# Routing two batches at once, every other iteration of the attention loop

## What is computed

```python
x = x + xattn(layernorm(x), ctx, mask, ...)      # q and o: quantized linear layers; k and v: plain
h = layernorm(x)                                 # 3584 tokens
probs = softmax(h @ router_w.T)                  # E = 8 experts
vals, idx = top_k(probs, 2); vals /= vals.sum()  # two experts for each token
x = x + sum over the two of vals * (silu(h @ gate.T) * (h @ up.T)) @ down.T
```

## Time and profile before

| | us |
|---|---|
| median of three runs | 1626.49 |
| the profiled execution | 1627.48 |
| its span (first to last instruction) | 1625.8 |
| PE busy | 1506.3 (93%) |
| DVE busy | 944.7 (58%) |
| ACT busy | 878.9 (54%) |
| POOL busy | 731.8 (45%) |
| mean granted clock of PE | 0.974 |

### The profile page before, as it was taken

The page is one execution under the profiler, slowest core; times in us unless marked ns, Lnnn a source line. Parts: engine busy times, 40 slices in busy tenths (PEclk is TensorE's granted clock), DMA queues, the critical chain, the costliest instruction groups (busy, mean ns, idle before and its releaser), DMA issues. The chain is left out here.

```text
span 1625.8 us, 40635 instructions
## 1 busy us (share of the span) xinstructions
PE 1506.3 (93%) x11593; PEld 1312.3 (81%) x11594; DVE 944.7 (58%) x2675; ACT 878.9 (54%) x2128; POOL 731.8 (45%) x798
## 2 busy tenths in 40 slices
PE   2899999999999999999999999995299999999796
PEld 2788888888888888888888888874299999999695
DVE  6567777777777777777777777765222222222121
ACT  2466666666666666666666666664033333333232
POOL 4234444543445434543444434542445555555352
PEclk9999999999999999999999999997599999999898
DMA  6667777677667777677766776668147766575543
GB/s 201 171 171 204 202 207 184 176 220 199 188 178 193 208 201 185 175 219 197 192 180 188 213 201 187 175 178 264 33 77 181 184 162 142 141 171 121 134 78 46
DMA packets 219151, 281.53 MB, mean 173 GB/s; under 512 B 82080, under 2 KB 163872, under 8 KB 219104
## 3 DMA queue, kind: packets, MB, share of 16 engines
q1 hardware_dynamic: 200928, 247.78, 54.2%
q0 software_dynamic: 18176, 33.17, 11.4%
HBM read 118.12 MB, written 66.77 MB: 114 GB/s over the span
## 5 line engine op out<-in xcount | busy, mean ns | idle before, releaser
L500 ACT ACTIVATE probs<-probs,neg_max 112x375 f32<-112x375 f32 x512 | 311.8, 609 | 235.2 <-DVE neg_max L576 229.1
L576 DVE CUSTOM_DVE_ANT_0 probs<-score,neg_mask 112x375 f32<-112x375 f32 x512 | 279.3, 545 | 195.9 <-PE score L729 179.7
L493 ACT ACTIVATE probs_t<-turn 125x336 f32<-125x336 f32 x512 | 225.0, 440 | 99.8 <-PE turn L737 99.4
L737 PE MATMUL turn<-ident,probs 112*125 112x112 f32 x1536 | 265.7, 282 | 2.7 <-ACT probs L500 2.7
L737 PEld LDWEIGHTS turn<-ident,probs 112*125 112x125 f32 x1536 | 223.6, 189 | 37.6 <-issue 19.1
L729 PE MATMUL score<-k_stack,q_stack 96*112 96x376 f32 x512 | 208.5, 407 | 4.3 <-DMA q_stack<-q_lo 3.4
L764 PE MATMUL proj<-down_hi,gate_up_hi 128*128 128x376 f32 x512 | 176.2, 344 | 14.9 <-DVE gate_up_lo L601 13.7
L978 POOL DMA_INDIRECT out<-y_rows,entries x63 | 102.2, 1622 | 175.0 <-ACT y_rows L1004 136.9
L1016 DVE TENSOR_TENSOR a_lo<-a_ps,a_hi 128x384 fp32r<-128x384 f32 x63 | 35.1, 558 | 250.9 <-ACT a_hi L991 159.0
L764 PE MATMUL proj<-down_hi,gate_up_lo 128*128 128x376 f32 x512 | 172.1, 336 | 0.0
L764 PE MATMUL proj<-down_lo,gate_up_hi 128*128 128x376 f32 x512 | 172.0, 336 | 0.0
(11 more groups left out here) (195 smaller groups left out, 3552.7 us busy)
## 6 DMA issues: line engine op xcount, KB each, us to landing
k_stack<-gate_up_hi SPq DMA_DIRECT2D x512, 94.0 KB, 2.1
k_stack<-gate_up_lo SPq DMA_DIRECT2D x256, 94.0 KB, 2.1
ctx_stage<-ctx_t SPq DMA_DIRECT2D x32, 750.0 KB
q_stack<-q_hi SPq DMA_DIRECT2D x256, 56.0 KB, 2.0
w_raw<-gate_up_t SPq DMA_DIRECT2D x32, 352.0 KB, 3.1
gate_up_dram_hi<-w_hi SPq DMA_DIRECT2D x32, 352.0 KB
gate_up_dram_lo<-w_lo SPq DMA_DIRECT2D x32, 352.0 KB
gate_up_hi<-gate_up_dram_hi SPq DMA_DIRECT2D x16, 704.0 KB, 6.6
```

Source lines behind the costliest of these rows:

```text
L493: act.activation(probs_t[:, h % RING_T, :, :], turn[h % 2][0:LC, 0:LT * N].rearrange("p (l n) -> p l n", l=LT), ACT.Copy).then_inc(turned_ ...
L500: act.activation(probs[:, h % DS, :], probs[:, h % DS, :], ACT.Exp, bias=neg_max[:, par % 2, h:h + 1], scale=-1.0, accum_out=total[:, par ...
L576: dve.tensor_tensor_reduce(probs[:, h % DS, :], score[h % 2][0:N, 0:L], neg_mask[:, p, :], 1.0, BIG, ALU.add, ALU.min, neg_max[:, p, h:h + ...
L737: mm = pe.transpose(turn[h % 2][0:LC, l * N:(l + 1) * N], probs[:, h % DS, l * LC:(l + 1) * LC], W["ident"][0:N, 0:N])
```

## The change

Routing is done for a pair of batches (an even one and the odd one after it) in the odd iterations. In each iteration DVE still finds the ordered logits and `equal` of its batch, now in one half of tiles that are twice as large. Everything behind that (L613 to L642 on DVE, L793 and L794 on PE, L439 to L482 on POOL, L541 on ACT) is left out of even iterations and done with twice the elements in odd ones. `taken_sum` now has two halves, the count before the even batch and the count before the odd one, so one more DVE addition stands at h = 8, behind `taken`. L619 and L634 compare with a broadcast tile in place of a scalar. The indirect DMAs aren't widened: an odd iteration issues four of them, an even one none. The two rank matmuls load 128 columns of weights in place of 112 and stream 16 columns in place of 8.

```diff
-                if has_m2:
-                    need(pool, routed, ROUTE * m2 + 1)
-                    need(pool, grown_made, m2)
-                    pool.tensor_tensor(gap[:, :], ordered[:, 1:2], ordered[:, 0:1], ALU.subtract).then_inc(weighing, 1)
+                if has_m2 and par % 2:
+                    need(pool, top_made, 2 * pair + 2)
+                    need(pool, grown_made, pair)
+                    pool.tensor_tensor(gap[:, :], ordered[:, :, 1], ordered[:, :, 0], ALU.subtract).then_inc(weighing, 1)
...
-                if has_m2:
...
-                    for i in range(2):
-                        pool.indirect_dma_start(slots, bass.IndirectOffsetOnAxis(ap=at[:, i:i + 1], axis=0), entry[:, i, :], None).then_inc(entered, 16)
+                if has_m2 and par % 2:
...
+                    for b in range(2):
+                        for i in range(2):
+                            pool.indirect_dma_start(slots, bass.IndirectOffsetOnAxis(ap=at[:, b, i:i + 1], axis=0), entry[:, b, i, :], None).then_inc(entered, 16)
...
-                    if h == 8 and has_m2:
-                        need(dve, routed, ROUTE * m2 + 6)
-                        dve.tensor_scalar(one[:, 1, :], W["prio"][0:N, :], best[1][:, 0:1], None, ALU.is_equal).then_inc(routed, 1)
-                        need(dve, routed, ROUTE * m2 + 7)
-                        need(dve, ranked, m2)
-                        dve.tensor_tensor(taken[0:N, :], one[:, 0, :], one[:, 1, :], ALU.add).then_inc(routed, 1)
-                    if h == 12 and has_m2:
-                        need(dve, routed, ROUTE * m2 + 9)
-                        need(dve, entered, 32 * m2)
-                        dve.tensor_reduce(at[:, :], chosen[:, :, :], AX.X, ALU.max).then_inc(routed, 1)
-                        dve.tensor_tensor(taken_sum[:, :], taken_sum[:, :], taken[0:N, :], ALU.add).then_inc(routed, 1)
+                    if h == 8 and has_m2 and par % 2:
+                        prio2 = W["prio"][0:N, :].unsqueeze(1).to_broadcast([N, 2, E])
+                        need(dve, routed, ROUTE * pair + 5)
+                        dve.tensor_tensor(one[:, :, 1, :], prio2, best[1][:, :].unsqueeze(2).to_broadcast([N, 2, E]), ALU.is_equal).then_inc(routed, 1)
+                        need(dve, routed, ROUTE * pair + 6)
+                        need(dve, ranked, pair)
+                        dve.tensor_tensor(taken[0:N, :, :], one[:, :, 0, :], one[:, :, 1, :], ALU.add).then_inc(routed, 1)
+                        need(dve, routed, ROUTE * pair + 7)
+                        dve.tensor_tensor(taken_sum[:, 1, :], taken_sum[:, 0, :], taken[0:N, 0, :], ALU.add).then_inc(routed, 1)
+                    if h == 12 and has_m2 and par % 2:
+                        need(dve, routed, ROUTE * pair + 9)
+                        need(dve, entered, 64 * pair)
+                        dve.tensor_reduce(at[:, :, :], chosen[:, :, :, :], AX.X, ALU.max).then_inc(routed, 1)
+                        dve.tensor_tensor(taken_sum[:, 0, :], taken_sum[:, 1, :], taken[0:N, 1, :], ALU.add).then_inc(routed, 1)
...
-                    if h == 11 and has_m2:
-                        need(pe, routed, ROUTE * m2 + 8)
+                    if h == 11 and has_m2 and par % 2:
+                        need(pe, routed, ROUTE * pair + 8)
                         if has_a:
                             need(pe, masked, it * H + h - 1)
-                        pe.matmul(rank[0:N, :], W["before"][0:N + 1, 0:N], taken[0:N + 1, :], start=True, stop=False)
-                        pe.matmul(rank[0:N, :], W["ones16"][0:N, 0:N], taken_sum[:, :], start=False, stop=True).then_inc(ranked, 1)
+                        pe.matmul(rank[:, :], W["before"][0:N + 1, :], taken[0:N + 1, :, :].rearrange("p b e -> p (b e)"), start=True, stop=False)
+                        pe.matmul(rank[:, :], W["ones16"][0:N, :], taken_sum[:, :, :].rearrange("p b e -> p (b e)"), start=False, stop=True).then_inc(ranked, 1)
```

More of the change, by code:

```diff
@@ L274, in attention @@
         NTP = NT + NT % 2
[L275 to L280, removed]
+        ordered, second = sb("ordered", [N, 2, E]), sb("second", [N, 2, E])
+        equal, weighed = sb("equal", [N, 2, 2, E]), sb("weighed", [N, 2, 2, E])
+        best = [sb(f"best{i}", [N, 2]) for i in range(2)]
+        one, taken, taken_sum = sb("one", [N, 2, 2, E]), W["taken"], W["taken_sum"]
+        chosen, at = sb("chosen", [N, 2, 2, E]), sb("at", [N, 2, 2], I32)
+        gap, grown, grown1 = sb("gap", [N, 2]), sb("grown", [N, 2]), sb("grown1", [N, 2])
+        entry = sb("entry", [N, 2, 2, 2], I32)
         cnt_i, tiles, last, jump = sb("cnt_i", [128, E], I32), sb("tiles", [128, E]), sb("last", [128, E]), sb("jump", [128, E])
@@ L283, in attention @@
         place_i = sb("place_i", [128, NTP], I32)
-        rank = score[1][:, LP:LP + E]
+        rank = score[1][:, LP:LP + 2 * E]
         o_bank, o_bank16 = proj[0], proj[1][:, :].bitcast(BF16)
@@ L416, in _, with body @@
         def _(pool):
-            def body(it, par, inside=False):
+            def body(it, par, pair, inside=False):
                 has_m2, has_m, has_a, has_n, has_nn, _ = stages(it, inside)
@@ L475, in body @@
[L475 to L479, removed]
+                    need(pool, weighing, WEIGH * pair + 4)
@@ L617, in body @@
[L617 to L623 removed]
+                        need(dve, routed, ROUTE * pair + 1)
@@ L699, in _ @@
             dve.wait_ge(counted, 1)
-            table(1, dve.tensor_scalar(cnt_i[:, :], rank[:, :], float(SLOTS - 1), float(SLOTS), ALU.add, ALU.max))
+            table(1, dve.tensor_scalar(cnt_i[:, :], rank[:, 0:E], float(SLOTS - 1), float(SLOTS), ALU.add, ALU.max))
             table(2, dve.tensor_scalar(cnt_i[:, :], cnt_i[:, :], 7, None, ALU.arith_shift_right))
@@ L856, in _ @@
             iterations(pe, body)
-            pe.wait_ge(routed, ROUTE * B)
-            pe.matmul(rank[:, :], W["ones16"][0:N, :], taken_sum[:, :], start=True, stop=True).then_inc(counted, 1)
+            pe.wait_ge(routed, ROUTE * B // 2)
+            pe.matmul(rank[:, 0:E], W["ones16"][0:N, :], taken_sum[:, 0, :], start=True, stop=True).then_inc(counted, 1)
 EXPERT_DMAS = 8
```

93 lines of the change are left out of this document (51 added, 42 removed).

## The result

The changed kernel took 1724.01 us (median of 4 runs, 1721.84 to 1737.63), beside 1627.39 for the kernel before: 1.061 times as long, with a 95% interval of 1.055 to 1.067. The forecast was 1670 with a range of 1640 to 1698. The sign was right and the size less than half of what was measured: +43 us predicted, +97 measured.

The account below looks back on a forecast made before the run. PE was taken to wait for `k_lo` behind POOL's DMAs. +2.6 us a pair gave +36.3 over 14 pairs; with -0.7 for early starts, -3.4 tail and +11 clock, +43 us: 1670 us, range 1640 to 1698.

Parts of the forecast that it names:

- What bounds the kernel: PE waits for DVE's `k_lo` 28 times, 13.7 us, behind POOL's DMAs; `o_int` has no slack before PE's turn.
- Two DMAs moved: Two more DMAs on POOL in odd iterations delay the next L425 by 2.68 us a pair; bounds 0 and 2.68.
- signs of being wrong: Wrong if L425 doesn't follow the DMAs, `k_lo` isn't PE's wait, or PE's period is no longer than before.
- DVE at head 8: New addition behind `taken` waits for POOL's L447, making `o_int` 1.25 us later; +0.3 us a pair, bounds 0 and 1.25.
- the two stalls don't add up: PE's 1.25 us stall at `o_int` and its later meeting with POOL's routing chain were not to be paid together.
- Wider operations on POOL: Entry operations on POOL with two elements a partition instead of one: +0.1 us a pair.
- Start of odd iterations: No DMA ahead of L425, so it starts 1.2 us sooner and `k_lo` is nearly in time: -0.35 us, bounds 0 and -0.55.
- PE −0.14 a pair: Even iterations lack the rank matmuls between PE's turn behind `values` and the score: -0.14 us, bounds -0.1 and -0.2.
- 128 columns nothing: Rank matmuls' weight loads on PE take 99 ns, not 136; at most 0.07 us ahead of a wait, so nothing.
- The tail: Iteration 33's L425 starts 4.87 us sooner, against four DMAs (+2.68 us): -3.4 us, bounds -2.2 and -4.7.
- The clock: PE's clock drops behind some waits at head 4 of even iterations: 0.8 us a pair, +11 us; bounds 0 and 3.4 a pair.
- no rival: Four alternatives: clock stays up, 1659 us (0.27); heavier, 1707 (0.08); DMAs don't hold L425, 1614 (0.07); half, 1641 (0.13).

Follow-up runs that it names:

- lower level: Runs of paired kernels in sets 2, 4 and 5, without late uptake of PE's results; the changed kernel took 1679.01 us (ratio 1.032).
- upper level: The first result and sets 1 and 3: ACT or DVE takes up a PE result over 1.5 us late once a pair; changed kernel 1724.01 us.
- sets 1 and 4: Groups of kernels run on one chip beside the kernel before, which took 1628.12 us in the first of them and 1625.51 in the other.

## Why the prediction was right or wrong

**What bounds the kernel: right.** A wait of PE behind POOL's queue, and `o_int` without slack. Moving the DMAs out of the way of the first gave 17 us; the earlier trace rows has 13.7.

**Two DMAs moved, +2.68 us a pair: right mechanism, wrong place in the sum.** The kernel before with doubled DMAs shows it: `x_s` 0.01 us behind the fourth, `k_lo` late by 3.05 us. The pitch was 1.25 us for the added ones, not 1.34. But in the changed kernel the term of 2.68 us is not paid in the pairs: `y` came after the DMAs. Two of the prediction's own signs of being wrong came true: L425 doesn't follow the DMAs, and `k_lo` isn't PE's wait.

**DVE at head 8, +0.3 us a pair: this is the step that failed.** The prediction had the addition's own wait right (1.18 us, ending with L449; 1.1 to 1.2 was forecast) and its way through `c_hi` and head 12 too. Counted from the start of the query bias, `o_int` starts 1.26 us later than before and `w_lo` 0.31 us later; the prediction had 1.25 and 0.3. It didn't put the two side by side. In before, `o_int` ran 0.3 us ahead of POOL's L461; with these two delays it starts behind L461's start, lasts 2.51 us in place of 0.43, and PE waits 3.2 us. So the stall of 1.25 us, which was the term's upper bound and was taken as mostly hidden, is one of 3.2 us, 15 times. The argument "the two stalls don't add up" was right; which of them is paid was reversed. The extra addition in the kernel before shows the cause by itself: 4.1 us an iteration.

The Trainium skill (SBUF — State Buffer, "SBUF: two separate sides") says that whichever of the two engines starts first has the shared ports for the whole instruction and the other blocks fully, and it counts operations in a 2-port mode among them, not only those with two inputs. `o_int` has one SBUF input; its 2.51 us agree with that half of the rule, which the prediction did not apply. Applied to the rows of before, with the prediction's delay of 0.3 us, `w_lo` ends at 921.59 + 0.3 + 2.47 = 924.36 and `o_int` not earlier, so that PE's turn of 921.33 is some 3.0 us late: an estimate, beside the measured 3.2.

**Wider operations on POOL, +0.1: small, as said.** From the end of `w_lo` to the first DMA it takes 2.75 us in before (924.06 to 926.81) and 2.96 in after (924.08 to 927.04).

**Start of odd iterations, −0.35: right in kind.** The waits for `k_lo` went from 28 to 2. In even iterations they went as well, which was not forecast.

**PE −0.14 a pair, 128 columns nothing:** the second is shown (ratio 0.999, interval 0.998 to 1.001). The first is too small to tell.

**The tail −3.4: right.** From the L425 of iteration 31 to that of 33 took 1140.57 − 1095.83 = 44.7 us; in after 1230.66 − 1188.73 = 41.9, and at the lower level 41.1. The table is done 16.2 to 16.3 us later in all three. So −2.8 and −3.6. In iteration 32 the sum's main mechanism is there: L427 starts 0.03 us behind the fourth DMA.

**The clock, +11: too small.** From 200 to 1080 us, 68 us at half speed are 34 us in after, and 55 are 27 at the lower level. Over the whole attention from 120 us on, and counting only the time in which PE was busy, it is 43 and 30 us more than in before. The prediction knew one such place and took 0.8 a pair; its upper bound of 3.4 held.

**The sum, made again.** The terms are waits of PE from the lists, after less before, and the prediction's own 2 us for PE. Lower level: 46.6 for `o_int` + 30 clock + (3.0 − 13.7) for `k_lo` − 2 − 3.6 tail = +60, measured +53.5. Upper level: 43.6 + 24.9 (the turn) + 43 + (4.9 − 13.7) − 2 − 2.8 = +98, measured +97. The spans of the profiled executions are 57 and 94 us longer. The terms aren't quite independent, so the sums are good to some 7 us, not better.

At the lower level the measured 1679 lies inside the forecast range of 1640 to 1698. That is luck: what carries the forecast's 2.6 us a pair is the DMA term of 2.68, which isn't paid, and in its place stands the `o_int` wait of 3.1 us a pair, which the sum has as 0.3.

**The third cause was in no rival.** It makes up 45 us between the two levels of one kernel, and is what puts the first result outside the range. It shows as PE's results taken up 2 to 3 us late at one place of the pair. Shown: it doesn't need a burst of four DMAs (they were split in two kernels that have it), nor the slow clock or the additions at heads 8 and 12 (one of these two has a single slow stretch and both additions moved). It was never seen in a kernel without pairs, though two of those ran in the sets at the upper level. It isn't bound to a chip: sets 1 and 4 ran on the same one, though no kernel with pairs ran in both.

One thing the traces show beyond this. In each of the seven upper-level traces the late uptake stands beside indirect DMAs on POOL: it mostly begins 1 to 5 us after the first DMA of a group starts and ends between 0.5 us before and 1.8 us after the end of the last one, and it moved with them, from the end of an iteration to head 5, when the DMAs were put behind `rstd2`. With the DMAs split two and two, only the group in the even iteration has it. So the DMAs are part of it or mark its place, though at the lower level the same DMAs at the same places come without it. Open: what it is. The kernel without the DMAs, the one with doubled DMAs and the one with PE's loop moved ran only at the lower level and so tell nothing on it.

## What to carry to other kernels

When an instruction is put in front of others on DVE, go down the engine's whole queue and ask of each one that runs shortly before a long POOL operation whether it will now start behind it: such a place jumps by the length of POOL's operation, not by the delay. If two waits of one engine lie within a period and on one chain, price each alone and expect to pay for one of them, and look for the fix in both at once, since one edit alone may gain nothing (the split DMAs) or lose (the one addition moved). Work that nobody waits for, like these DMAs, belongs behind the last operation of the queue that the critical engine needs; that alone, without the change, gave 1%.

## What the runs showed of the hardware

- An addition of 8 elements on DVE took 1.18 to 1.33 us while POOL ran in after, and 0.16 us where it was moved away from POOL's operations (set 1). A f32 to bf16 operation of 112x512 with one input took 2.51 in place of 0.43 us. Both ended with POOL's operation or 0.3 us behind. A reduction of 112x512 on DVE (L685), 0.69 us, was not held up inside POOL's L458.
- In an otherwise full PE, waits of about 3 us were followed by the 1.2 GHz level for 3.4 to 10.2 us. From 200 to 1080 us: 24 waits and 24 slow stretches with the DMAs doubled (2.0 us lost a wait), 23 and 23 with the extra addition (1.7), 12 and 12 in after at the lower level (2.3).
- Indirect DMAs of 112 rows of 8 bytes started 1.25 us apart in POOL's queue (1.34 to 1.52 from the first to the second).
- Two kernels had two levels 39 and 45 us apart, each steady within a set of runs, while the kernel before stayed within 3 us. A difference of 2% between kernels from different sets should be taken again in one.
